# FFN weights as one-byte integers, cast to bf16 by every load, with the zero point taken out by a rank-1 product

## The chip, the cores and the metric

The kernel runs on all 8 NeuronCores of one Trainium2 chip. Each core computes one batch element on its own (2048 tokens of 2048 features), with the same weights. The metric is the device time of the slowest core in microseconds. Cores 0 to 3 are one die, cores 4 to 7 the other. The profile is one execution, read on its slowest core, core 1.

## The reference

One transformer layer with the norm behind each part. B = 8, S = E = 2048, 16 heads, 5632 hidden units. Weights of the FFN are integers 0 to 255 held as int32, with a zero point of 128 and a scale per output row.

```python
# attention (latent kv of 128, 64 plain + 64 rotary dims a head), causal
out  = softmax((q_nope @ k_nope.T + q_rope @ k_rope.T) / sqrt(128)) @ v
x    = layernorm(x + out.reshape(B, S, 2048) @ W_o)
# FFN
def qlinear(x, wq, scale):
    return x @ ((wq.astype(float32) - 128.0) * scale[:, None]).T
h    = silu(qlinear(x, wq_gate, s_gate)) * qlinear(x, wq_up, s_up)
x    = layernorm(x + qlinear(h, wq_down, s_down))
```

## The kernel before

Everything is held transposed: features on the 128 partitions, tokens along the row. The kernel goes through the tokens in four tiles of 512 (`ti` = 0 to 3). A small scheduler, `Sched`, appends each step to a list per engine, with the semaphore counts it waits for; an engine's list is replayed strictly in the order in which the Python code made it. The engines are "t" TensorE (PE), "v" VectorE (DVE), "s" ScalarE (ACT), "g" GpSimd (POOL) and "q" SyncE (SP). DMAs stand in the lists of the engines that issue them: SP and ACT use the hardware queues, POOL the software queue. All matrix products are recorded in one helper (L163), so the profile tells them apart by their tiles.

Preparation (0 to 198 us): small weights are loaded as float32 and cast; `W_o` is cast to bf16 and written to the DRAM scratch `wo_b`.

Each tile then has these stages.

- Start (`emit_astart`, made at the end of the tile before, ahead of its second layer norm). POOL loads x for the tile into `C` as bf16 in two DMAs (L315, from float32), each of 8 x 512 columns; PE makes the latent kv, the latent query and the rotary key from it (`SA<-C,w_dkv` first), then the 16 heads' queries.
- Attention, head by head. For each pair of key blocks, PE puts scores into the PSUM bank pair `SA` or `SB` (on the diagonal with a mask product), ACT takes the exp into `AR` (L545), and PE multiplies it with v into `O` and with ones into `SM` for the row sum. The next head's keys and values are made in between (`KV`, L267, L295). Tile `ti` has 2 (`ti` + 1) pairs a head.
- In tile 0 only, three pieces of `wd` are made ready at the start of every head, 48 in all (`mk_wd_part`). SP loads a piece of up to 2048 columns of int32 into `B` (`B<-wd`, 1024 KB), one buffer for all pieces; DVE (L478, pieces 0 and 2 of a row) or ACT (L481, piece 1) subtracts 128 and writes bf16; ACT issues the store to the scratch `wd_b` (L490). These steps stand in the engines' lists ahead of the head's own exps.
- Output projection from `wo_b`, residual, first layer norm. Its result is in `A` (float32) and in `C` (bf16, cast in four parts by L789).
- Gate/up: 44 chunks `hc` of 128 hidden units, 16 products each for gate and for up, into `SA` and `SB` in turn. L903 is the silu, L912 the product with up, which writes `H[hc]` in `AR`. The weights of a chunk, 128 x 2048 each, have two buffers each in `AR`. In tile 0 POOL loads them from int32 with a cast to bf16 in the DMA (`AR<-wg`, `AR<-wu`, L813 and L819), DVE subtracts 128 in place (L825, L832), and ACT writes them to the scratches `wg_b` and `wu_b`; a buffer is free when both its products and its store are done. In tiles 1 to 3 SP loads bf16 from the scratches.
- Down: 16 groups `ec` of 44 products into `O0` and `O1` in turn. The 5632 columns of a group's weights lie in `AR` in two halves. They are loaded in four pieces: pieces 0 and 1 (2048 and 768 columns) once product 21 of the group before is done, pieces 2 and 3 (1280 and 1536) once that group is. Products 0, 16, 22 and 32 wait for pieces 0 to 3. In all tiles SP loads them from `wd_b` (L938). DVE adds the residual (L966).
- Second layer norm, and the store of y.

`m128b` (one row of -128) and `rowb` (one row of 512, bf16) are there before, and nothing reads them.

Of the kernel before, what the change touches and what calls it, by code (L numbers as in the profile page):

```python
# [9 lines left out]
I32 = mybir.dt.int32  # L10

S = 2048
# [68 lines left out]
def build_program(nc):  # L81
# [11 lines left out]
    wg = nc.dram_tensor("wg", [NHC, 128, NEC * 128], I32, kind="ExternalInput")  # L93
    wu = nc.dram_tensor("wu", [NHC, 128, NEC * 128], I32, kind="ExternalInput")
    wd = nc.dram_tensor("wd", [NEC, 128, NHC * 128], I32, kind="ExternalInput")
# [8 lines left out]
    wg_b = nc.dram_tensor("wg_b", [NHC, 128, NEC * 128], BF16, kind="Internal")  # L104
    wu_b = nc.dram_tensor("wu_b", [NHC, 128, NEC * 128], BF16, kind="Internal")
    wd_b = nc.dram_tensor("wd_b", [NEC, 128, NHC * 128], BF16, kind="Internal")
# [4 lines left out]
    with ExitStack() as ctx:  # L111
# [3 lines left out]
        def ps(name):  # L115
# [32 lines left out]
                     "Dp0", "Dp1", "Dp2", "Dst0", "Dst1", "Dst2", "Dst3",  # L148
                     "Dsg0", "Dsg1", "Dsu0", "Dsu1", "Dsd0", "Dsd1",
                     "Dwo0", "Dwo1", "Dg0", "Dg1", "Du0", "Du1",  # L150
                     "Dd0", "Dd1", "Dy"]
# [4 lines left out]
        pi = [B[:, i * 2048:(i + 1) * 2048].bitcast(I32) for i in range(4)]  # L156
# [65 lines left out]

        piQ = [B[:, i * 2048:(i + 1) * 2048].bitcast(I32) for i in range(4)]
        poQ = B[:, 6144:8192].bitcast(BF16)
        conv_tok = {}
# [17 lines left out]
        tok_expt_rd = [None, None]  # L243
        t_hc_last = None
# [187 lines left out]
        for ti in range(NT):  # L432
# [26 lines left out]
            wd_parts = []  # L459
            if ti == 0:  # L460
                cstate = {"q2": [t for t in half_free if t is not None],
                          "po0": None, "po1": None,
                          "st_wg0": None, "st_wg1": None,
                          "st_wu0": None, "st_wu1": None, "blast": []}

                def mk_wd_part(row, part):
                    def run():
                        w0 = part * 2048
                        n = min(2048, NHC * 128 - w0)
                        t_ld = sc.dma(  # L470
                            "q",
                            lambda q, row=row, w0=w0, n=n: q.dma_start(
                                piQ[2][:, 0:n], wd[row, :, w0:w0 + n]),
                            deps=[cstate["q2"]], inc="Dp0")
                        po = poQ[:, (part % 2) * 2048:(part % 2) * 2048 + n]
                        t_cv = sc.st(
                            "v" if part % 2 == 0 else "s",
                            (lambda v, po=po, n=n: v.tensor_scalar(  # L478
                                po, piQ[2][:, 0:n], -128.0, None, ALU.add))
                            if part % 2 == 0 else  # L480
                            (lambda s, po=po, n=n: s.activation(  # L481
                                po, piQ[2][:, 0:n], AF.Identity,
                                bias=np.float32(-128.0))),
                            deps=[t_ld, cstate["po%d" % (part % 2)]],
                            inc="V" if part % 2 == 0 else "S")
                        cstate["q2"] = t_cv
                        t_st = sc.dma(
                            "s",
                            lambda s, row=row, w0=w0, n=n, po=po:
                            s.dma_start(wd_b[row, :, w0:w0 + n], po),  # L490
                            deps=[t_cv], inc="Dsd%d" % (part % 2))
                        cstate["po%d" % (part % 2)] = t_st
# [631 lines left out]
```

How the kernel before makes its waits and increments, by code:

```python
    def replay(self, eng_name, eng, sems):  # L52
        wm = {}
        for fn, waits, inc, amt in self.steps[eng_name]:
            for (sname, val) in waits:
                if wm.get(sname, 0) < val:
                    eng.wait_ge(sems[sname], val)
                    wm[sname] = val
            inst = fn(eng)
            if inc is not None:
                inst.then_inc(sems[inc], amt)
```

## Time and profile before

| | us |
|---|---|
| median of 2 runs | 4304.75 (4299.38 to 4310.12) |
| the profiled execution, its own time | 4291.6 |
| its span, core 1 | 4290.1 |
| the eight cores' spans | 4260.5 to 4290.1 |
| mean granted clock of the cores | 0.877 to 0.880 of full speed |

The span is the time from the first to the last instruction of the slowest core. In the page and in the answers, a row such as `O<-AR` says what is written and what is read; a releaser behind `<-` is what ended an engine's wait. For a DMA, the row gives the KB written and the time from its issue to its landing. A DMA queue's share is the time that its packets took, as a part of the 16 DMA engines' time.

### The profile page before, as it was taken

To read this page: it belongs to the slowest core of one execution; us is meant where nothing else is said; L and a number is where in the kernel's file an instruction comes from. 1 tells how busy PE (TensorE), PEld (TensorE's weight loads), DVE (VectorE), ACT (ScalarE), POOL (GpSimd) and SP (SyncE) were. 2 spreads that over 40 slices of the span, in tenths; PEclk is the share of its full clock that TensorE was granted. 3 is DMA by queue.
4 is the path that set the end of the run, shared out by engine and by line. 5 is a ranking of instruction groups with operands and counts; after the bars stand their busy time and mean duration, and the time that the engine had idled before them with its cause. 6 is when DMAs were issued, how large, how long until landed. Compare 5 with 4: busy or idle time off the path is not lost.

```text
span 4290.1 us, 35670 instructions; the slowest of 8 cores (4260.5 to 4290.1 us)
## 1 busy us (share of the span) xinstructions
PE 3250.2 (76%) x13312; PEld 1235.0 (29%) x13312; DVE 859.9 (20%) x1275; ACT 846.4 (20%) x985; POOL 56.4 (1%) x100
## 2 busy tenths in 40 slices
PE   0133337677789578799996688799995788889996
PEld 0000002233334122344442122344441222334442
DVE  1031111322211422311004321311004222121102
ACT  1122222100000243210002444210002455211000
POOL 0000000011100000000000000000000000000000
PEclk9955558899999688899997888899996898989998
DMA  6634444699973200344540201344540200234442
GB/s 217 184 119 162 161 162 131 148 216 210 212 185 110 78 2 20 103 152 152 157 150 13 79 1 34 104 152 152 160 144 0 79 1 1 98 118 152 148 150 101
DMA packets 154950, 505.71 MB, mean 118 GB/s; under 512 B 15136, under 2 KB 31648, under 8 KB 147616
## 3 DMA queue, kind: packets, MB, share of 16 engines
q1 hardware_dynamic: 103648, 354.51, 25.2%
q0 software_dynamic: 20992, 54.53, 8.4%
q10 hardware_dynamic: 30144, 94.38, 5.7%
q8 instruction: 112, 1.84, 0.2%
q14 instruction: 54, 0.44, 0.0%
HBM read 463.52 MB, written 94.37 MB: 130 GB/s over the span
## 4 chain that ended last, share of the span: by engine, by line
PE 62%; DMA 19%; DVE 9%; ACT 5%; issue 4%; DVEq 0%; ACTq 0%; SPq 0%; POOL 0%; POOLq 0%
PE O L163 18%; PE SA L163 17%; PE SB L163 16%; PE SM L163 8%; DMA B<-wd 4%; DMA AR<-wu 4%; DMA wu_b<-AR 4%; PE KV L163 3%; DVE A L767 2%; ACT AR L545 2%; DMA B<-wo 1%; DMA wo_b<-C 1%; DVE AR L409 1%; DVE B L775 1%; DMA AR<-wo_b 1%
## 5 line engine op out<-in xcount | busy, mean ns | idle before, releaser
L163 PE MATMUL O<-AR 128*128 128x512 bf16 x3456 | 840.4, 392 | 339.7 <-ACT AR L545 327.2
L163 PE MATMUL SA<-C,AR 128*128 128x512 bf16 x2816 | 647.5, 388 | 135.9 <-DVE AR L825 68.0
L163 PE MATMUL SB<-C,AR 128*128 128x512 bf16 x2816 | 628.7, 381 | 48.2 <-DVE AR L825 45.3
L163 PEld LDWEIGHTS O<-AR 128*128 128x128 bf16 x3456 | 335.8, 100 | 797.3 <-issue 439.2
L163 PEld LDWEIGHTS SA<-C,AR 128*128 128x128 bf16 x2816 | 276.6, 99 | 500.1 <-issue 189.6
L163 PEld LDWEIGHTS SB<-C,AR 128*128 128x128 bf16 x2816 | 274.7, 98 | 391.5 <-issue 70.0
L163 PE MATMUL SA<-AR 128*128 128x512 bf16 x832 | 256.6, 425 | 58.7 <-DVE AR L295 52.9
L163 PE MATMUL SM<-AR,onesb 128*1 128x512 bf16 x640 | 227.6, 443 | 60.9 <-DVE AR L611 60.9
L545 ACT ACTIVATE AR<-SA 128x1024 bf16<-128x1024 f32 x160 | 164.0, 1025 | 415.0 <-PE SA L163 220.5
L163 PE MATMUL SB<-AR 128*128 128x512 bf16 x832 | 234.6, 396 | 9.3 <-DMA AR<-wo_b 5.0
L295 DVE CAST AR<-KV 128x512 bf16<-128x512 f32 x160 | 110.7, 692 | 471.8 <-PE KV L163 471.8
L903 ACT ACTIVATE AR<-SB,sgT 128x512 bf16<-128x512 f32 x88 | 60.7, 689 | 602.8 <-PE SB L163 565.1
L545 ACT ACTIVATE AR<-SB 128x1024 bf16<-128x1024 f32 x160 | 163.0, 1019 | 77.5 <-PE SB L163 74.1
L903 ACT ACTIVATE AR<-SA,sgT 128x512 bf16<-128x512 f32 x88 | 60.7, 689 | 590.5 <-PE SA L163 465.9
L912 DVE SCALAR_TENSOR_TENSOR AR<-SA,suT,AR 128x512 bf16<-128x512 f32 x88 | 66.1, 751 | 515.5 <-PE SA L163 515.5
L912 DVE SCALAR_TENSOR_TENSOR AR<-SB,suT,AR 128x512 bf16<-128x512 f32 x88 | 66.1, 751 | 507.8 <-PE SB L163 507.8
L163 PE MATMUL SA<-C,w_dkv 128*128 128x512 bf16 x64 | 18.0, 441 | 194.6 <-DMA C<-x 194.6
L966 DVE SCALAR_TENSOR_TENSOR B<-O,sdT,A 128x512 f32<-128x512 f32 x64 | 48.1, 751 | 577.8 <-PE O L163 577.8
L163 PEld LDWEIGHTS SA<-AR 128*128 128x128 bf16 x832 | 76.2, 102 | 192.3 <-issue 138.6
L267 ACT CAST AR<-KV 64x512 bf16<-64x512 f32 x160 | 91.6, 573 | 176.6 <-PE KV L163 176.6
L611 DVE COPY AR<-SM 128x512 f32<-128x512 f32 x64 | 44.3, 692 | 361.7 <-PE SM L163 361.7
L163 PE MATMUL SM<-rows,onesf 1*128 1x512 f32 x128 | 85.0, 749 | 36.0 <-ACT rows L596 36.0
(90 smaller groups left out, 1717.1 us busy)
## 6 DMA issues: line engine op xcount, KB each, us to landing
AR<-wg_b SPq DMA_DIRECT2D x132, 512.0 KB, 3.3
AR<-wu_b SPq DMA_DIRECT2D x132, 512.0 KB, 3.3
B<-wd SPq DMA_DIRECT2D x32, 1024.0 KB, 6.3
AR<-wo_b SPq DMA_DIRECT2D x64, 512.0 KB, 3.3
AR<-wd_b SPq DMA_DIRECT2D x64, 512.0 KB, 3.8
AR<-wd_b SPq DMA_DIRECT2D x64, 384.0 KB, 3.7
AR<-wg POOLq DMA_DIRECT2D x44, 512.0 KB, 9.0
AR<-wu POOLq DMA_DIRECT2D x44, 512.0 KB, 9.7
```

The lines of the kernel that those rows point to most:

```text
L163: t.matmul(o, l, r, start=a, stop=b),
L267: lambda s, khs=khs, c5=c5: s.copy(AR[0:64, khs + c5 * 512:khs + (c5 + 1) * 512], KV[0:64, :]),
L295: lambda v, vts=vts, tg=tg: v.tensor_copy(AR[:, vts + tg * 512:vts + (tg + 1) * 512], KV[:, :]),
L409: lambda v, ssl=ssl, b=Pb: v.tensor_tensor(scrB, b[64:128, :], ssl, ALU.mult),
L545: lambda s, SC=SC, etb=etb: s.activation(AR[:, etb:etb + 1024], SC[:, 0:1024], AF.Exp, scale=np.float32(QSCALE)),
L611: "v", lambda v: v.tensor_copy(sbinv, SM[:, :]),
L767: lambda v, ec2=ec2: v.tensor_tensor(dst_f32[:, ec2 * 512:(ec2 + 1) * 512], src_f32[:, ec2 * 512:(ec2 + 1) * 512], O0[:, :], ALU.subtract),
L775: lambda v, ec2=ec2, out_t=out_t: v.tensor_tensor(out_t[:, ec2 * 512:(ec2 + 1) * 512], dst_f32[:, ec2 * 512:(ec2 + 1) * 512], O1[:, :], AL ...
L903: lambda s, hc=hc, pgb=pgb, gsil_o=gsil_o: s.activation(AR[:, gsil_o:gsil_o + 512], pgb, AF.Silu, scale=sgT[:, hc:hc + 1]),
L912: v.scalar_tensor_tensor(AR[:, AR_H + hc * 512:AR_H + (hc + 1) * 512], pub, suT[:, hc:hc + 1], AR[:, gsil_o:gsil_o + 512], ALU.mult, ALU.m ...
L966: lambda v, ec=ec, pbd=pbd: v.scalar_tensor_tensor(B[:, ec * 512:(ec + 1) * 512], pbd[:, :], sdT[:, ec:ec + 1], A[:, ec * 512:(ec + 1) * 512],
```

## The change

The host hands over `wg`, `wu` and `wd` as uint8. The scratches `wg_b`, `wu_b` and `wd_b`, the 48 `wd` steps of tile 0's attention and the DVE subtractions are gone. In all four tiles POOL loads gate, up and down weights with a cast from uint8 to bf16 in the DMA, in one list in the order of use, and the products are made with the raw 0 to 255.

For gate and up nothing takes the place of the subtraction: their input is the output of the layer norm, whose features add up to zero for each token, so a constant of 128 in every weight adds nothing (up to rounding). For down the zero point is taken off with the column sums of `H`: 44 products with a column of ones add them up in `SM[0:1]` (one ahead of each chunk from chunk 2 on, two behind the last), ACT copies them as bf16 to `rowb`, and a rank-1 product of `m128b` and `rowb` closes each of the 16 groups of the down stage.

```diff
-    wg = nc.dram_tensor("wg", [NHC, 128, NEC * 128], I32, kind="ExternalInput")
+    wg = nc.dram_tensor("wg", [NHC, 128, NEC * 128], U8, kind="ExternalInput")
...
-                for _ in range(3):
-                    if wd_parts:
-                        wd_parts.pop(0)()
...
-                if ti == 0:
-                    t_gl = sc.dma(
-                        "g",
...
-                else:
-                    t_gl = sc.dma(
-                        "q",
...
+                t_gl = sc.dma(
+                    "g",
+                    lambda g, hc=hc, gb=gb: g.dma_start(
+                        AR[:, AR_GS[gb]:AR_GS[gb] + 2048],
+                        wg[hc, :, :]),
+                    deps=[t_g_free[gb]], inc="Dg%d" % gb)
...
+                if hc >= 2:
+                    MM(SM[0:1, :], onesb[:, :],
+                       AR[:, AR_H + (hc - 2) * 512:AR_H + (hc - 1) * 512],
+                       hc - 2 == 0, False,
+                       [t_H[hc - 2]] + ([tok_pb["SM"]] if hc == 2 else []))
...
+            t_cs = MM(SM[0:1, :], onesb[:, :],
+                      AR[:, AR_H + 43 * 512:AR_H + 44 * 512], False, True,
+                      [t_H[43]], inc="T")
+            t_rowb = sc.st(
+                "s", lambda s: s.copy(rowb[0:1, :], SM[0:1, :]),
+                deps=[t_cs, tok_rowb_free], inc="S")
...
                     hw[p] = sc.dma(
-                        "q",
-                        lambda q, ec=ec, c0=c0, c1=c1: q.dma_start(
-                            AR[:, c0:c1], wd_b[ec, :, c0:c1]),
-                        deps=pc_dep[p] + [t_d_free[p // 2]]
-                             + (store_tok[("wd_b", ec)] if ti <= 1 else []),
+                        "g",
+                        lambda g, ec=ec, c0=c0, c1=c1: g.dma_start(
+                            AR[:, c0:c1], wd[ec, :, c0:c1]),
+                        deps=pc_dep[p] + [t_d_free[p // 2]],
                         inc=pc_sem[p])
...
+                t_dm = MM(pbd[:, :], m128b[0:1, :], rowb[0:1, :],
+                          False, True, [t_rowb], inc="T")
```

ScalarE, one head of tile 0's attention before (L545 the exps, L591 and L596 the inverse of the row sum, L490 the stores to `wd_b`):

```order
L490 DMA wd_b<-B 128x2048 [waits semV]
L481 ACTIVATE B<-B 128x2048 [waits semDp0,semDsd1]
L490 DMA wd_b<-B 128x2048 [waits semS]
L490 DMA wd_b<-B 128x1536 [waits semV]
L545 ACTIVATE AR<-SA 128x1024 [waits semT]
L591 ACTIVATE rows<-SM 1x512
L596 ACTIVATE rows<-rows 1x512 [waits semS]
L267 CAST AR<-KV 64x512 [waits semT]
L545 ACTIVATE AR<-SB 128x1024 [waits semT]
```

The same head after the change (L494 is now the exp, L540, L545 and L261 the other three):

```order
L494 ACTIVATE AR<-SA 128x1024 [waits semT]
L540 ACTIVATE rows<-SM 1x512
L545 ACTIVATE rows<-rows 1x512 [waits semS]
L261 CAST AR<-KV 64x512 [waits semT]
L494 ACTIVATE AR<-SB 128x1024 [waits semT]
```

The four steps for `wd` ahead of the first exp are gone, the rest stands as it was.

POOL, at the end of tile 0's FFN, before: the last load of `wu`, then x for the tiles 1, 2 and 3 with nothing between.

```order
L819 DMA AR<-wu 128x2048 [waits semT,semDsu1]
L315 DMA C<-x 128x8x512 [waits semV]
L315 DMA C<-x 128x8x512
L315 DMA C<-x 128x8x512 [waits semV]
L315 DMA C<-x 128x8x512
```

After: the last two groups of the down weights of tile 0 (L844), x for tile 1 (L309), and the first weights of tile 1 (L758, L764).

```order
L844 DMA AR<-wd 128x2048 [waits semT]
L844 DMA AR<-wd 128x768
L844 DMA AR<-wd 128x1280 [waits semT]
L844 DMA AR<-wd 128x1536
L309 DMA C<-x 128x8x512 [waits semV]
L309 DMA C<-x 128x8x512
L758 DMA AR<-wg 128x2048 [waits semT]
L764 DMA AR<-wu 128x2048
```

The loads of x now stand behind all 64 pieces of the tile's down weights.

PE, from the last chunk of gate/up into the first down group, after the change (`SM<-AR,onesb` is a column sum of `H`, `O<-rowb,m128b` the rank-1 product):

```order
L159 MATMUL SB<-C,AR 128x512 [waits semDu1]
L159 MATMUL SB<-C,AR 128x512 x15
L159 MATMUL SM<-AR,onesb 1x512 [waits semV] x2
L159 MATMUL O<-AR 128x512 [waits semDd0]
L159 MATMUL O<-AR 128x512 x15
L159 MATMUL O<-AR 128x512 [waits semDd1]
L159 MATMUL O<-AR 128x512 x5
L159 MATMUL O<-AR 128x512 [waits semDd2]
L159 MATMUL O<-AR 128x512 x9
L159 MATMUL O<-AR 128x512 [waits semDd3]
L159 MATMUL O<-AR 128x512 x11
L159 MATMUL O<-rowb,m128b 128x512 [waits semS]
```

Before, the same place has the 32 products of the chunk and then the 44 of the group, without the two column sums and the last row.

## Rows read from the trace of the kernel before

**Rows 1.** The page, part 4: the chain that ended last, shares by line.
```profile
PE O L163 18%; PE SA L163 17%; PE SB L163 16%; PE SM L163 8%; DMA B<-wd 4%; DMA AR<-wu 4%; DMA wu_b<-AR 4%; PE KV L163 3%; DVE A L767 2%; ACT AR L545 2%; DMA B<-wo 1%; DMA wo_b<-C 1%; DVE AR L409 1%; DVE B L775 1%; DMA AR<-wo_b 1%
```

**Rows 2.** Table of stretches: length, busy us (instructions) per engine, granted clock, DMA share, GB/s.
```profile
249.00:678.00 429.00, 158.31 (x362) 35.01 (x362) 70.19 (x91) 85.82 (x94) 0.00 (x0) 0.58 0.48 162
...
777.00:1210.00 433.00, 329.02 (x1409) 136.78 (x1410) 89.52 (x130) 32.87 (x46) 46.89 (x84) 0.96 0.96 210
...
1802.00:2106.00 304.00, 303.66 (x1398) 137.25 (x1399) 32.35 (x44) 31.84 (x46) 0.00 (x0) 0.99 0.44 148
...
4079.00:4231.00 152.00, 152.00 (x706) 68.79 (x704) 12.02 (x16) 0.00 (x0) 0.00 (x0) 1.00 0.43 145
```

**Rows 3.** Waits of PE and ACT in tile 0's attention: us in total, times, longest.
```profile
PE O L163 <- ACT AR L545: 238.1, 16, 16.7
...
ACT B L481 <- DMA B<-wd: 215.4, 16, 14.0
ACT AR L545 <- DVE B L478: 119.3, 16, 7.8
```

**Rows 4.** Timeline of one head in tile 0: start us, us, engine, line.
```profile
576.44 1.91 ACT L481 ACTIVATE B<-B 128x2048 bf16<-128x2048 int32 x1 [13.85 <-DMA B<-wd]
...
584.18 0.96 DVE L478 TENSOR_SCALAR B<-B 128x1536 bf16<-128x1536 int32 x1 [14.47 <-DMA B<-wd]
585.68 1.02 ACT L545 ACTIVATE AR<-SA 128x1024 bf16<-128x1024 f32 x1 [7.33 <-DVE B L478]
...
586.85 1.01 PE L163 MATMUL O<-AR 128*128 128x512 bf16 x2 [15.93 <-ACT AR L545]
```

**Rows 5.** Timeline around the ends of gate/up, tiles 0 and 1.
```profile
776.36 1.91 ACT L789 ACTIVATE C<-A 128x2048 bf16<-128x2048 f32 x1 [3.65 <-DVE A L775]
...
777.12 9.61 PE L163 MATMUL SA<-C,AR 128*128 128x512 bf16 x32 [23.29 <-DVE AR L825]
...
1209.81 9.66 PE L163 MATMUL O<-AR 128*128 128x512 bf16 x44
...
1800.29 1.91 ACT L789 ACTIVATE C<-A 128x2048 bf16<-128x2048 f32 x1 [3.65 <-DVE A L775]
...
2105.59 1.67 PE L163 MATMUL O<-AR 128*128 128x512 bf16 x7
2105.93 0.75 DVE L912 SCALAR_TENSOR_TENSOR AR<-SB,suT,AR 128x512 bf16<-128x512 f32 x1 [6.16 <-PE SB L163]
```

**Rows 6.** POOL's loads: queues from 780 to 1210 us, tile wg, 736.8 to 739.2.
```profile
q0 software_dynamic: 12096, 44.05, 68.2%
q10 hardware_dynamic: 12435, 45.24, 27.7%
...
L813 POOL DMA_DIRECT2D AR<-wg x44: 528/528/853, 736.8 to 1192.4; - x44
...
DMA to landing us min/median/max: 5.2/9.0/13.9
...
DMA packets 0, 0.00 MB, mean 0 GB/s; under 512 B 0, under 2 KB 0, under 8 KB 0
...
AR<-wg POOLq DMA_DIRECT2D x1, 512.0 KB, 6.9
```

**Rows 7.** Waits of PE; down stage of tile 3; SP's issue; packets from 2169 to 2170.6.
```profile
PE O L163 <- DMA AR<-wd_b: 12.5, 6, 5.1
...
AR<-wd_b SPq DMA_DIRECT2D x15, 512.0 KB, 3.9
...
2169.27 0.79 SPq L938 DMA_DIRECT2D AR<-wd_b  x2
...
q1 hardware_dynamic: 3, 0.01, 4.8%
```

**Rows 8.** Timeline, a run of products with one column of weights.
```profile
1768.68 3.62 PE L163 MATMUL KV<-AR,onesb 128*1 128x512 bf16 x16
```

**Rows 9.** DMA queues from 3060 to 3085 us, x for tile 3.
```profile
q0 software_dynamic: 2080, 2.10, 52.7%
```

More of the change, by code:

```diff
@@ L10 @@
 I32 = mybir.dt.int32
+U8 = mybir.dt.uint8
 S = 2048
@@ L457, in build_program @@
                     deps=tok_A_free, inc="Dx%d" % (2 + j)))
-            wd_parts = []
-            if ti == 0:
[L461 to L470, printed above, removed]
-                            "q",
[L472 to L492, printed above, removed]
-                        store_tok.setdefault(("wd_b", row), []).append(t_st)
-                        cstate["blast"] = [t_cv, t_st]
-                    return run
-                for row in range(NEC):
-                    for part in range(3):
-                        wd_parts.append(mk_wd_part(row, part))
             pending_tail = None
@@ L666, in build_program @@
                     deps=[t_mm, t_xr[ec // 8]]
-                         + (tok_B_free if ec == 0 else [])
-                         + (cstate["blast"] + [cstate["q2"], cstate["po0"],
-                                               cstate["po1"]]
-                            if ec == 8 and ti == 0 else []), inc="V")
+                         + (tok_B_free if ec == 0 else []), inc="V")
                 tok_pb[wn] = t_add
@@ new lines, in build_program @@
+                t_gl = sc.dma(
[4 more added lines that the diff above has]
+                    deps=[t_g_free[gb]], inc="Dg%d" % gb)
+                t_ul = sc.dma(
+                    "g",
+                    lambda g, hc=hc, gb=gb: g.dma_start(
+                        AR[:, AR_US[gb]:AR_US[gb] + 2048],
+                        wu[hc, :, :]),
+                    deps=[t_u_free[gb]], inc="Du%d" % gb)
@@ L894, in build_program @@
                 ums.append(t_um)
-                if ti == 0:
-                    t_g_free[gb] = [t_gm, st_g]
-                    t_u_free[gb] = [t_um, st_u]
-                else:
-                    t_g_free[gb] = t_gm
-                    t_u_free[gb] = t_um
+                t_g_free[gb] = t_gm
+                t_u_free[gb] = t_um
                 t_sil = sc.st(
@@ L957, in build_program @@
                               AR[:, AR_H + hc * 512:AR_H + (hc + 1) * 512],
-                              hc == 0, hc == NHC - 1, d,
-                              inc="T" if hc in (21, NHC - 1) else None)
+                              hc == 0, False, d,
+                              inc="T" if hc == 21 else None)
                     if hc == 21:
                         t_d_free[0] = t_dm
+                t_dm = MM(pbd[:, :], m128b[0:1, :], rowb[0:1, :],
+                          False, True, [t_rowb], inc="T")
+                tok_rowb_free = t_dm
                 t_d_free[1] = t_dm
@@ L1063, in _host_layouts @@
         wo.reshape(16, 128, 16, 128).transpose(2, 1, 0, 3).reshape(16, 128, 2048))
-    wgq = np.asarray(inputs["L0_ffn_wq_gate"], np.int32).T
+    wgq = np.asarray(inputs["L0_ffn_wq_gate"], np.int32).astype(np.uint8).T
     d["wg"] = np.ascontiguousarray(
         wgq.reshape(16, 128, 44, 128).transpose(2, 1, 0, 3).reshape(44, 128, 2048))
-    wuq = np.asarray(inputs["L0_ffn_wq_up"], np.int32).T
+    wuq = np.asarray(inputs["L0_ffn_wq_up"], np.int32).astype(np.uint8).T
     d["wu"] = np.ascontiguousarray(
         wuq.reshape(16, 128, 44, 128).transpose(2, 1, 0, 3).reshape(44, 128, 2048))
-    wdn = np.asarray(inputs["L0_ffn_wq_down"], np.int32).T
+    wdn = np.asarray(inputs["L0_ffn_wq_down"], np.int32).astype(np.uint8).T
     d["wd"] = np.ascontiguousarray(
```

97 lines of the change are left out of this document (14 added, 83 removed).

## The prediction

> **What bounds the kernel now.** I read the page first, its chain that ended last. The products of TensorE (PE, line L163) lead it, but `B<-wd`, `AR<-wu` and `wu_b<-AR` stand in it with 4% of the span each, 12% together [rows 1]. All three belong to the dequantisation, so the next view is the table of stretches, to see where PE has holes [rows 2]. Gate/up of tile 0 takes 433 us with the 16 DMA engines at 0.96, where the same matmuls take about 304 us with DMA at 0.44 in tile 1. Attention of tile 0 takes 429 us with PE busy for 158. The down products are packed (152 of 152 us in tile 3).
>
> The waits of PE in tile 0's attention name one thing: 238.1 us, 16 times, once a head, until the exp of L545 [rows 3]. ScalarE itself is late because it stands at L481 for the `wd` load (215.4 us) and then, in the first exp, for L478 (119.3 us) [rows 3]. The timeline of one head shows it: L481 begins at 576.44 when its load has landed, the second store sits on ScalarE's queue until L478 has run at 584.18, and the exp starts at 585.68 [rows 4]. So attention of tile 0 is bounded by three serial load-convert rounds a head.
>
> **What goes.** (a) The 48 `wd` rounds. The 16 waits of 238.1 us go. What is late next is the exp itself, which lets PE go 1.17 us after its own start (585.68 to 586.85), most of it under the other bank's score products; I leave 0.4 us of wait a head, 6.4 us. A head is 429 / 16 = 26.8 us now, so 26.8 - 15.9 = 10.9 us without the wait of the row, at a granted clock of 0.58 of full speed on average [rows 2, 4]. With fewer holes the clock should be higher, so a little comes on top: 238 - 6 + 6 = **238 us**, between 225 and 256.
>
> (b) Gate/up of tile 0. I measure from one anchor, the last cast of the normalised tile (L789), to the first down product: 776.36 to 1209.81 is 433.5 us in tile 0, 1800.29 to 2105.59 is 305.3 us in tile 1 [rows 5]. The int32 load plus the bf16 write-back fill the engines: 68.2% + 27.7% of 430 us [rows 6]. That is 430 x 0.682 / 84 = 3.49 us of all 16 engines a load and 430 x 0.277 / 86 = 1.39 a store; two of each make 9.76 us a chunk, where PE needs 6.91 (32 products at 0.216). With the stores, the L825/L832 steps and three quarters of the source bytes gone, tile 0 runs as tile 1: **-128 us**.
>
> (c) PE waits 12.5 us in all for `wd_b` pieces at the start of the down stage [rows 7], while in tiles 0 to 2 x for the next tile is loaded beside them (in tile 3, without it, PE is busy throughout [rows 2]). The x load moves away: **-12.5 us**, at worst 0.
>
> **What comes.** (d) 44 column-sum products and 16 rank-1 products a tile, 240 in all. One-column products of this width stand 3.62 us for 16, less the tail of the last [rows 8]: 0.216 us each, the same as a full one (44 in 9.66 with the last one's tail, [rows 5]). Nothing hides them, since PE is packed here: 240 x 0.216 = **+52 us**.
>
> (e) The last column sum needs `H[43]`. L912 begins 0.34 us after the last up product is over and takes 0.75 [rows 5]; before, 43 down products lay over this. About 1 us, 4 times: **+4 us**. The row copy on ScalarE has the whole first down group as cover (9.5 us).
>
> (f) Loads of the gate/up stage leave SP's hardware queue for POOL's software queue, with the cast in the DMA. POOL issues one in 0.53 us [rows 6]. Each buffer is free for three half chunks, 10.4 us, before it is needed. A landing of 6.9 us (software, first pair, [rows 6]) is hidden. Even if the cast still cost 3.49 us a load, two would take 6.98 us of a chunk's 6.91 + 0.22 = 7.13. **0 us**, at most some 20.
>
> (g) The down stage has much less cover. Pieces 0 and 1 of the next group can be issued when product 21 is done, and piece 0 is needed after 22 more products and the rank-1 one: 23 x 0.216 = 4.97 us. The time from one group to the next is thus at least 4.75 us plus the landing. The hardware queue lands piece 0 in 3.9 us in tile 3 [rows 7], where PE is busy throughout [rows 2]. The software queue starts later: its first load was issued at 736.8, no packet moved until 739.2 (2.4 us) and it landed after 6.9 [rows 6]; on SP, issued at 2169.27, the first packets are there before 2170.6 (under 1.3 us) [rows 7]. That is 1.1 us or a little more between the two, 1.2. So 3.9 + 1.2 + 0.1 for the semaphores = 5.2 us, if uint8 to bf16 costs what a bf16 load of as many written bytes costs. Bounds: 3.9 (nothing lost) to 6.9 us (the int32 load of 1 MB in the first pair). I take 5.2, since the bytes written are those of the rows of the down stage. Lost: 4.75 + 5.25 - 9.72 = 0.3 us a group, 63 groups: **+19 us**; with the bounds 0 and 123 us.
>
> The Trainium skill, DMA: Bandwidth & Descriptors, section "Anatomy of one DMA", gives about 2.0 us plus bytes / 436e3 for a software-queue DMA, 3.2 us for piece 0. By that, (g) would be 0 and the sum 19 us lower. The trace does not agree: 2.4 us passed before the first packet. The same page (section "Latency and other measured facts") puts the software queue's first byte only 0.4 us behind the hardware one; the rows have 1.2 us between them.
>
> (h) `C<-x` of the next tile was issued as soon as `H[43]` was there, and lay under the whole down stage. Now its two DMAs stand on POOL behind 64 `wd` pieces, and the last two of these wait for the end of group 14. They go out two issues of 0.53 us, 1.1 us, into group 15. PE's next work (L163 `SA<-C,w_dkv`) is behind group 15 and needs the first half of x, then the second. With nothing else moving, the pair for tile 3 took 52.7% of 16 engines over 25 us, 13.2 us of transfer [rows 9]. Counted from the start of group 15: 1.1 + 2.4, one more for pieces 2 and 3 in front, then 13.2 to 15: the second half is there at 18 to 20 us, and PE would have needed it at 9.7 + 1.7 = 11.4. Three times about 8 us, 24. After such a hole the clock is at its lower level for a while: after the 23 us hole at 777.12 a run of 32 products took 9.61 us where 32 x 0.216 + 0.15 is 7.06 [rows 5], 2.6 us more. **+32 us**, between 15 and 45.
>
> **The sum** against the profiled execution (span 4290.1, its own time 4291.6): -238 - 128 - 12.5 + 52 + 4 + 0 + 19 + 32 = -271.5, so 4020 us. The two runs shown have a median 13 us above the profiled one; with part of that I say **4030 us**. HBM traffic falls (each weight is read as one byte, never written), but no row shows HBM as a limit outside tile 0, so I book nothing for it.
>
> **Rivals.** *The cast costs by element.* If the DMA engines spend the same time on 262,144 elements whether these are int32 or uint8, a load stays at 3.49 us, where the bf16 loads of tile 1 take 0.44 x 304 / 88 = 1.52 [rows 2]. For: only 4-byte sources are cast in this trace, and nothing shows one with a 1-byte source. Against: bytes read explain 3.49 as well (1 MB). Then (f) holds at its edge and piece 0 lands at about 6.3 us: 4.75 + 6.35 - 9.72 = 1.4 us a group, 87 in place of 19: **4098 us**.
>
> *The software queue keeps its slow landing* (median 9.0 us [rows 6]) in the down stage. Then a group takes 4.75 + 9.0 = 13.8 us, 4 more than now, 255 us in all: **4266 us**, within 2%. This is also the way to a slower kernel: place, the down stage; price, 63 us for each us of landing over 4.97; from a landing of about 9.6 us nothing is left of the gain, and the 13.9 us that is the row's maximum would end at **4577 us**. For: same queue, same engine. Against: these 9 us were taken with DMA at 0.96, with stores and int32 sources that are gone; in the down stage the share is about 0.43.
>
> *Attention of tile 0 does not shrink*, because the wait only changes hands. For: ScalarE carries the exps, and the waits of one engine are rarely due to one other alone. If only half of the 238 us came back: **4150 us**. Against: all three parties of the wait are removed instructions.
>
> **How the numbers follow.** Forecast 0.72, cast by element 0.15, half of attention's gain 0.05, slow landing at 9 us 0.04, slower still 0.02, something better (no late x, no late piece, near 3980) 0.02. A change of about 2% is what can be told from none here. Faster by over 2% (below 4219): 0.72 + 0.15 + 0.05 + 0.02 + a little = 0.95; within 2%: 0.03; slower: 0.02. The range of 3975 to 4125 takes in the element rival and the bounds of (g) and (h).
>
> **What would show it.** In the profile after: tile 0's attention at some 11 us a head with no `B<-wd`; gate/up of every tile 6.91 + 0.22 us a chunk; PE waits for `AR<-wd` small and many (0.3 us x 60) or, for the element rival, 1.4 us each; PE waits for `C<-x` three times 6 to 10 us before `SA<-C,w_dkv`. If DMA's share in gate/up of tile 1 is near 0.45 the cast goes by bytes, near 0.98 by elements. I am wrong if the software queue lands pieces later than 6.9 us, or if tile 0's heads stay above 15 us.

## The result, and the profile after

The changed kernel takes 3995.66 us (median of 11 executions) against 4305.76 us (10 executions) for the kernel before. The ratio is 0.9285, 95% interval 0.9264 to 0.9306: 7% faster. The forecast was 4030 us, with a range of 3975 to 4125 us; the median lies in it. Ratios are taken from executions in which no die ran at a lower granted clock than the other; where the chip showed that in most executions of a kernel (e7), single undisturbed ones are named instead.

The page's first line and its chain that ended last, by line (changed kernel):
```profile
span 3991.4 us, 35128 instructions; the slowest of 8 cores (3964.9 to 3991.4 us)
...
PE SA L159 22%; PE SB L159 20%; PE O L159 19%; PE SM L159 10%; PE KV L159 4%; DVE A L713 2%; DMA C<-x 2%; ACT AR L494 2%; DVE AR L289 1%; DMA B<-wo 1%; DMA wo_b<-C 1%; DVE AR L403 1%; DVE A L721 1%; DVE B L721 1%; DVE AR L560 1%
```

The three transfers that held 12% of the chain [rows 1] are gone from it. Of the DMA that is left there, `wo` and 27 us of `C<-x` belong to the start of the kernel, which the change does not touch. The rest of `C<-x` is new: the chain runs through a load of x at the start of each of the tiles 1, 2 and 3 (14.8, 14.7 and 14.0 us), which is term (h).

The table of stretches, changed kernel (columns as in [rows 2]): attention of tile 0, gate/up of tile 0, gate/up of tile 1, down of tile 3:
```profile
246.00:405.80 159.80, 124.30 (x353) 32.30 (x357) 35.19 (x59) 55.30 (x78) 0.00 (x0) 0.72 0.02 7
501.50:826.80 325.30, 320.74 (x1413) 137.42 (x1443) 33.03 (x44) 33.51 (x47) 46.51 (x88) 0.99 0.41 141
1423.00:1748.40 325.40, 320.78 (x1413) 137.45 (x1443) 33.02 (x44) 33.53 (x47) 46.53 (x88) 0.99 0.41 140
3773.30:3931.90 158.60, 157.74 (x706) 68.94 (x720) 11.26 (x15) 0.53 (x1) 31.79 (x60) 1.00 0.42 137
```

Tile 0's attention, up to the first product of the output projection (405.82 us), is down from 429 to 160 us, 10.0 us a head, and its gate/up from 433 to 325 [rows 2]. But gate/up of tile 1 went up from 304 to 325, with PE busy for 320.8 of it, and down of tile 3 from 152 to 158.6, with PE busy for 157.7. These two rows say that the added products cost more than their number times 0.216 us. The timeline of PE shows how:

Timeline of PE, changed kernel, two chunks in tile 0, the end of gate/up, and two down groups of tile 3 (start us, us, engine, line):
```profile
788.50 0.38 PE L159 MATMUL SM<-AR,onesb 128*1 128x512 bf16 x1
788.81 7.08 PE L159 MATMUL SB<-C,AR 128*128 128x512 bf16 x31
...
795.82 0.38 PE L159 MATMUL SM<-AR,onesb 128*1 128x512 bf16 x1
...
826.25 0.38 PE L159 MATMUL SM<-AR,onesb 128*1 128x512 bf16 x1 [0.77 <-DVE AR L811]
826.78 8.58 PE L159 MATMUL O<-AR 128*128 128x512 bf16 x39 [0.16 <-issue]
...
3911.65 0.39 PE L159 MATMUL O<-rowb,m128b 1*128 1x512 bf16 x1
3911.97 9.67 PE L159 MATMUL O<-AR 128*128 128x512 bf16 x43
3921.57 0.39 PE L159 MATMUL O<-rowb,m128b 1*128 1x512 bf16 x1
```

From one column sum to the next are 795.82 - 788.50 = 7.32 us, where 32 products take 6.91 us: 0.41 us for the one that was added. (The records hold 31 of the 32 here, so the period is the thing to read, not the count.) From one rank-1 product to the next are 3921.57 - 3911.65 = 9.92 us where 44 products take 9.50: 0.42 us. The wait of 0.77 us at 826.25 is term (e).

The waits of PE in two stretches (us in total, times, longest), and the tiles `wd` and `wg`, changed kernel; first the largest of PE in tile 0's attention, then the whole from 200 us on:
```profile
PE SM L159 <- DVE AR L560: 15.1, 15, 1.0
...
PE SA L159 <- DMA C<-x: 15.5, 6, 3.2
...
PE SM L159 <- DVE AR L811: 3.1, 4, 0.8
...
DMA to landing us min/median/max: 2.3/3.3/4.7
...
DMA to landing us min/median/max: 3.1/3.4/3.8
```

The 238.1 us until the exp [rows 3] are gone altogether: no row of PE in tile 0's attention names the exp. No row of PE names `AR<-wd` either: the four pieces of the down weights together land in 3.3 us (median, at most 4.7) and are never waited for. `C<-x` is waited for twice at each of the three tile starts.

Where the time went, stage by stage, in the two profiled executions (anchors as in the prediction, [rows 5]):

| stretch | before | after | difference | forecast |
|---|---|---|---|---|
| up to the use of the second half of x in tile 0 | 198.2 | 194.5 | -3.6 | 0 |
| tile 0: start, attention, projection, norm | 578.2 | 307.0 | -271.2 | -238 |
| tile 0: gate/up | 433.5 | 325.3 | -108.2 | -128 + 9.5 + 1 |
| tiles 1 to 3: gate/up | 915.2 | 973.9 | +58.7 | 28.5 + 3 |
| four down stages | 626.1 | 634.6 | +8.5 | -12.5 + 13.8 + 19 |
| tiles 1 to 3: attention, with the wait for x; tail | | | +17 | +32 |

(28.5 is 3 x 44 x 0.216, 13.8 is 64 x 0.216.) The differences add up to -299, as the spans do: 4290.1 - 3991.4 = 298.7. The first row is work that the change leaves alone. Of the second row, 269 us lie ahead of the output projection; from the first product of the projection to the end of the norm it is 98.0 us before and 95.7 after.

### The profile page after: what moved, and what is told of

Read it like the earlier page. It is cut to its first block, busy times and chain, and to the rows that moved or that the text cites. A ratio compares the mean times of both kernels' runs of the same rounds, so it can differ in the third digit from the quotient of the medians.

```text
span 3991.4 us, 35128 instructions; the slowest of 8 cores (3964.9 to 3991.4 us)
## 1 busy us (share of the span) xinstructions
PE 3274.0 (82%) x13289; PEld 1236.0 (31%) x13552; DVE 766.8 (19%) x1155; ACT 817.2 (20%) x973; POOL 329.2 (8%) x620
## 4 chain that ended last, share of the span: by engine, by line
PE 75%; DVE 9%; DMA 6%; ACT 5%; issue 4%; DVEq 0%; POOL 0%; ACTq 0%; another core or an unknown queue 0%; SPq 0%; POOLq 0%
PE SA L159 22%; PE SB L159 20%; PE O L159 19%; PE SM L159 10%; PE KV L159 4%; DVE A L713 2%; DMA C<-x 2%; ACT AR L494 2%; DVE AR L289 1%; DMA B<-wo 1%; DMA wo_b<-C 1%; DVE AR L403 1%; DVE A L721 1%; DVE B L721 1%; DVE AR L560 1%
## 5 line engine op out<-in xcount | busy, mean ns | idle before, releaser
L159 PE MATMUL O<-AR 128*128 128x512 bf16 x3376 | 828.3, 388 | 95.4 <-ACT AR L494 89.0
L159 PE MATMUL SA<-C,AR 128*128 128x512 bf16 x2756 | 639.3, 387 | 80.5 <-ACT C L735 77.8
L159 PE MATMUL SB<-C,AR 128*128 128x512 bf16 x2760 | 620.1, 379 | 2.9
L159 PEld LDWEIGHTS SA<-C,AR 128*128 128x128 bf16 x2816 | 271.2, 99 | 430.5 <-issue 130.0
L159 PE MATMUL SM<-AR,onesb 128*1 128x512 bf16 x816 | 289.3, 422 | 65.3 <-DVE AR L560 60.5
L159 PE MATMUL SA<-AR 128*128 128x512 bf16 x803 | 246.0, 420 | 64.0 <-DVE AR L289 52.2
L758 POOL DMA_DIRECT2D AR<-wg x176 | 93.1, 529 | 2409.6 <-PE SA L159 2106.4
L494 ACT ACTIVATE AR<-SA 128x1024 bf16<-128x1024 f32 x160 | 163.9, 1024 | 393.8 <-PE SA L159 318.1
L844 POOL DMA_DIRECT2D AR<-wd x256 | 135.5, 534 | 526.3 <-PE O L159 477.6
L494 ACT ACTIVATE AR<-SB 128x1024 bf16<-128x1024 f32 x160 | 162.8, 1018 | 76.8 <-PE SB L159 76.5
L159 PEld LDWEIGHTS SM<-AR,onesb 128*1 128x1 bf16 x816 | 42.9, 80 | 320.8 <-issue 320.8
```

Of the source, the lines that this page charges most:

```text
L159: t.matmul(o, l, r, start=a, stop=b),
L494: lambda s, SC=SC, etb=etb: s.activation(AR[:, etb:etb + 1024], SC[:, 0:1024], AF.Exp, scale=np.float32(QSCALE)),
L758: lambda g, hc=hc, gb=gb: g.dma_start(AR[:, AR_GS[gb]:AR_GS[gb] + 2048], wg[hc, :, :]),
L844: lambda g, ec=ec, c0=c0, c1=c1: g.dma_start(AR[:, c0:c1], wd[ec, :, c0:c1]),
```

## The experiments

Two theories stood against each other at first. Mine: the gain is two separate things, the `wd` rounds and the engines' load in gate/up, and the price is what the added products cost on a packed PE. The rivals: the gains hang together (one saves nothing without the other), or the price lies in the software queue or in late x.

Where a run is so many us below the changed kernel, its median is taken from 3995.66 us. The two were not always timed side by side, so the difference of their ratios to the kernel before, in us and with its interval, stands beside it where it matters.

**e1: the down weights alone.** They come as uint8 through POOL, the `wd` rounds are gone; gate and up are converted as before.

```
-    wg = nc.dram_tensor("wg", [...], U8, ...)
+    wg = nc.dram_tensor("wg", [...], I32, ...)
...
+    wg_b = nc.dram_tensor("wg_b", [NHC, 128, NEC * 128], BF16, kind="Internal")
...
+                if ti == 0:
+                    t_g_free[gb] = [t_gm, st_g]
```

> The kernel before with the down weights alone changed: uint8 cast on load by POOL, no wd rounds in tile 0's attention; gate/up as before (int32, -128 on DVE, scratches), no column sums and no rank-1 products, so the zero point of the down weights is left out. Theory (terms read from the profile after): attention of tile 0 -260 us, output projection and norm of tile 0 -11 us, the waits for wd_b pieces -12, late x +20: about 4305 - 263 = 4042 us, ratio 0.939. Rival, the sizes of the prediction: -238 - 12.5 + 19 + 32 = -200, 4105 us, ratio 0.953.

Measured: 4032.23 us, ratio 0.9396 (0.9362 to 0.943). Table of stretches of e1, attention and gate/up of tile 0:
```profile
246.00:408.00 162.00, 129.59 (x360) 33.08 (x357) 35.20 (x59) 55.26 (x78) 0.00 (x0) 0.69 0.02 7
524.00:948.00 424.00, 320.73 (x1356) 133.08 (x1355) 87.85 (x126) 28.97 (x43) 47.55 (x86) 0.95 0.97 210
```
Attention of tile 0 shrinks as far as in the changed kernel (the stretch of 162 us against 429) while gate/up stays at 424 us with the engines at 0.97. So the `wd` rounds are a gain by themselves. The ratio meets the expectation (0.939); its rival, the sizes of the prediction (0.953), lies outside the interval.

**e2: gate and up alone.** They come as uint8 through POOL in all tiles; the `wd` rounds and the bf16 copy of `wd` stay.

```
-    wd = nc.dram_tensor("wd", [NEC, 128, NHC * 128], U8, kind="ExternalInput")
+    wd = nc.dram_tensor("wd", [NEC, 128, NHC * 128], I32, kind="ExternalInput")
...
+                for _ in range(3):
+                    if wd_parts:
+                        wd_parts.pop(0)()
```

> The kernel before with the gate/up weights alone changed: uint8 cast on load by POOL in all tiles, no subtraction on DVE, no scratches for them; the wd rounds in tile 0's attention and the down stage as before. Theory: gate/up of tile 0 falls to the 305 us of tile 1, -128 us, all else stays: 4177 us, ratio 0.970. Rival: the software queue costs something in tiles 1 to 3 (cast by element, landing over 10.4 us), then gate/up there is longer than 305 us and the ratio is above 0.98.

Measured: ratio 0.9707 (0.9616 to 0.9798); the profiled execution has 4146.6 us. Table of stretches of e2, gate/up of tile 0 and tile 1:
```profile
775.00:1080.60 305.60, 302.62 (x1368) 137.29 (x1397) 32.28 (x43) 32.88 (x46) 44.38 (x84) 0.99 0.44 147
1668.00:1972.00 304.00, 301.74 (x1367) 137.04 (x1396) 32.27 (x43) 32.16 (x46) 44.38 (x84) 0.99 0.44 148
```
Its waits of PE still hold the exps, 310.5 us in 69 waits where the kernel before has 327.2 in 72. Tile 0's gate/up, from the last cast to the first down product, needs 306.2 us (774.46 to 1080.64) in place of 433.5: -127 us, term (b) as forecast. Tile 1, where only the queue changed (POOL with a cast in place of SP), stays at 304: term (f), nothing, is right too. The two halves are independent, and the spans of the profiled executions say so once more: e1 is 4290.1 - 4036.8 = 253 us shorter than the kernel before and e2 143.5 us, 397 together, and the whole change without its added products (e3, below) is 396 us shorter.

**e3: without the added products.** Column sums and rank-1 products are left out, and with them the zero point of the down weights.

```
-                    MM(SM[0:1, :], onesb[:, :],
-                       AR[:, AR_H + (hc - 2) * 512:AR_H + (hc - 1) * 512],
...
-                t_dm = MM(pbd[:, :], m128b[0:1, :], rowb[0:1, :],
-                          False, True, [t_rowb], inc="T")
```

> The changed kernel without its 44 column sums and 16 rank-1 products a tile; the zero point of the down weights is left out. Theory: each inserted product costs 0.41 us with the switch to another shape and back, so 240 of them 98 us, and the wait for H[43] 4: about 3894 us, ratio to before 0.905. Rival (the prediction's price, 0.216 us each): 52 + 4 = 56 us, about 3940 us, ratio 0.915.

Measured: 3894.53 us, ratio 0.9076 (0.9046 to 0.9107), 101 us below the changed kernel; by the ratios 90 us, 16 either way, by the two profiled spans 97. The rival's 56 us is out. The wait for `H[43]` went with the products, so of the 101 us some 94 are theirs, about 0.4 us each and not 0.216. Gate/up of tile 0 in e3:
```profile
507.00:812.00 305.00, 302.89 (x1395) 136.93 (x1396) 32.26 (x43) 33.48 (x46) 46.52 (x88) 0.99 0.44 148
```

**e4: the column sums in one run.** The same 44 products, all behind the last up product and not one in each chunk.

```
-            MM(SM[0:1, :], onesb[:, :],
-               AR[:, AR_H + 42 * 512:AR_H + 43 * 512], False, False,
...
+            for hc in range(NHC):
+                t_cs = MM(SM[0:1, :], onesb[:, :],
+                          AR[:, AR_H + hc * 512:AR_H + (hc + 1) * 512],
```

> The changed kernel with all 44 column sums of a tile in one run behind the last chunk, in place of one ahead of each chunk; same products, same result. Switch theory (the extra 0.2 us is paid where the shape or the bank changes, about 0.1 at each end): 44 in a run stand at 0.216, so 42 x 0.2 x 4 = 33 us less than the changed kernel, about 3963 us, chunk period 6.91. Rival, shape theory (a one-column product itself costs 0.41 in this stage): nothing changes, 3996 us. What the wait for H[43] was stays.

Measured: 3954.16 us, ratio 0.9218 (0.9197 to 0.9239), 41 us below the changed kernel with the same number of products (by the ratios 29 us, 13 either way, so clear of the rival's nothing). Timeline of PE in e4:
```profile
799.75 7.07 PE L159 MATMUL SB<-C,AR 128*128 128x512 bf16 x32
806.75 9.66 PE L159 MATMUL SM<-AR,onesb 128*1 128x512 bf16 x44
816.34 9.67 PE L159 MATMUL O<-AR 128*128 128x512 bf16 x44
825.94 0.39 PE L159 MATMUL O<-rowb,m128b 1*128 1x512 bf16 x1
```
The 44 take 9.6 us, 0.22 each. Back to back with their like they cost what I had charged; it is the single one among others that costs 0.41. From 7.07 us for 32 to the next start are 7.00, not 6.91, and 9.59 for 44 in place of 9.50: each change of shape costs some 0.1 us. One part of the expectation missed: the wait for `H[43]` did not stay. No idle time stands in the run of 44, whose first 43 need only earlier chunks. Gate/up of the four tiles is 39 us shorter in all, 33 from the changes of shape and 6 from this.

**e5: the rank-1 product at full height.** `rowb` and `m128b` get 128 rows (127 of `rowb` zero), so that the closing product has the shape of the others.

```
-        m128b = sb("m128b", [1, 128], BF16)
-        rowb = sb("rowb", [1, 512], BF16)
+        m128b = sb("m128b", [128, 128], BF16)
+        rowb = sb("rowb", [128, 512], BF16)
...
-                t_dm = MM(pbd[:, :], m128b[0:1, :], rowb[0:1, :],
+                t_dm = MM(pbd[:, :], m128b[:, :], rowb[:, :],
```

> The changed kernel with the product that closes a down group in full shape: 128 rows of -128 as weights and a 128-row operand that is zero but for its first row, so the same result. Shape theory for the closing product: a product on one row costs 0.42 us in a run of full ones, a full one 0.216, so a group falls from 9.92 to 9.72 us and the kernel by 64 x 0.2 = 13 us, about 3983 us. Rival: the cost lies in what follows it (the wait for rowb, the change of bank between groups, which groups had before too), then a group stays at 9.92 us.

Measured: 3986.52 us, ratio 0.9252 (0.921 to 0.9294), 9 us below the changed kernel. Timeline of PE in e5:
```profile
3906.20 0.38 PE L159 MATMUL O<-rowb,m128b 128*128 128x512 bf16 x1
3906.42 9.66 PE L159 MATMUL O<-AR 128*128 128x512 bf16 x44
3915.91 0.38 PE L159 MATMUL O<-rowb,m128b 128*128 128x512 bf16 x1
```
A group is 9.71 us, not 9.92: the closing product is 0.2 us cheaper with 128 rows than with one. 64 x 0.2 is 13 us. The total alone could not show it: the medians are 9 us apart, the ratios 14 us with 20 either way. The groups also change between the PSUM banks `O0` and `O1`, and 9.71 us is 45 x 0.216, so the change of bank adds nothing here. So of the 0.42 us half is the product and half the change of shape.

**e6: the down weights as int32.** Same program, only the source type differs: every `wd` piece reads four times the bytes.

```
-    wd = nc.dram_tensor("wd", [NEC, 128, NHC * 128], U8, kind="ExternalInput")
+    wd = nc.dram_tensor("wd", [NEC, 128, NHC * 128], I32, kind="ExternalInput")
```

> The changed kernel with the down weights as int32 again, cast by the load: same bytes written, four times the bytes read, so that the landing of piece 0 gets longer in the quiet down stage. Packets of such a cast took 324 ns in the gate/up stage before, against 175 ns now from uint8. By the prediction's relation for a group (4.75 us + landing + a little): with a landing of 3.5 + 1.375 x 8 x 0.15 = 5.2 us, a group takes 10.0 to 10.2 us in place of 9.92, PE waits 0.1 to 0.3 us a group, 6 to 18 us in all, about 4005 us. Rival 1: software queue slow whenever the source is int32 (2.4 us to the first packet, landing 6.9 as in the first pair before): group 11.7 us, 1.8 x 63 = +112, about 4108 us. Rival 2: the source's width costs nothing: 3996 us.

Measured: ratio 0.9546 (0.9461 to 0.9631), the profiled execution 4115.7 us. Down stage of tile 3 in e6, its landings, its waits, and a piece of its timeline:
```profile
3872.00:4056.00 184.00, 162.03 (x721) 68.95 (x720) 11.26 (x15) 0.58 (x1) 31.70 (x60) 0.99 0.72 120
...
AR<-wd POOLq DMA_DIRECT2D x15, 512.0 KB, 5.6
...
PE O L159 <- DMA AR<-wd: 88.6, 68, 2.9
...
4011.95 9.66 PE L159 MATMUL O<-AR 128*128 128x512 bf16 x44 [1.23 <-DMA AR<-wd]
4023.07 4.91 PE L159 MATMUL O<-AR 128*128 128x512 bf16 x22 [1.14 <-DMA AR<-wd]
4029.35 1.02 PE L159 MATMUL O<-AR 128*128 128x512 bf16 x4 [1.37 <-DMA AR<-wd]
```
A group takes 184 / 16 = 11.5 us, and the price against the changed kernel is 4115.7 - 3991.4 = 124 us. By my relation (4.75 us plus the landing of piece 0) a landing of 5.6 us gives 10.4 us a group, and the expectation worked out on it was missed. The relation counts only the first pair of pieces; the timeline shows PE waiting in the second half of a group too, since the pair behind lands late as well. So the relation is a lower bound. The waits for pieces name 88.6 us of the 119 by which the four down stages grew; for the rest nothing is named. The rival's total comes near the measured one, but by another route: piece 0 lands after 5.6 us, and the second pair adds waits of its own. The experiment shows two things: the landing is the term that decides in the down stage, as the slow rivals had it, and the small source is what kept the changed kernel away from it.

**e7: x in pieces between the down groups.** One sixteenth of x behind each group's four `wd` pieces, and not two large DMAs behind all of them.

```
+                if ti + 1 < NT:
+                    t_x1 = sc.dma(
+                        "g",
+                        lambda g, ec=ec, q1=(ti + 1) * TT: g.dma_start(
+                            C[:, ec * 512:(ec + 1) * 512], ...
```

> The changed kernel with x for the next tile loaded in 16 blocks, one behind the four pieces of each down group, in place of two DMAs behind all 64 pieces. Theory: PE's two waits for C<-x at the start of tiles 1 to 3 (15.5 us in all) and the run at the lower clock behind them go, 20 us together, while a block of 0.5 us of transfer a group is hidden under the pieces: about 3976 us. Rival: each block delays the pieces behind it and PE waits for AR<-wd again, by up to 0.5 us a group, 24 us over three tiles: 3996 us or above.

Measured: 3981.7 and 3982.2 us in its two undisturbed executions, 14 us below the changed kernel; the spans of the profiled executions, 3980.6 and 3991.4, are 11 us apart. Timeline of PE at the start of tile 1, and waits of PE, in e7:
```profile
989.73 0.39 PE L159 MATMUL O<-rowb,m128b 1*128 1x512 bf16 x1
990.05 3.63 PE L159 MATMUL SA<-C,w_dkv 128*128 128x512 bf16 x16
...
PE SA L159 <- DMA C<-x: 192.1, 2, 187.5
PE O L159 <- DMA AR<-wd: 4.0, 3, 1.3
```
In the changed kernel the same place reads:
```profile
985.27 0.38 PE L159 MATMUL O<-rowb,m128b 1*128 1x512 bf16 x1
987.92 1.89 PE L159 MATMUL SA<-C,w_dkv 128*128 128x512 bf16 x8 [2.27 <-DMA C<-x]
...
992.98 2.69 PE L159 MATMUL SA<-C,w_dkv 128*128 128x512 bf16 x8 [3.17 <-DMA C<-x]
995.46 4.55 PE L159 MATMUL SA<-C,w_dq 128*128 128x512 bf16 x15
999.84 2.32 PE L159 MATMUL SB<-C,w_krp 128*128 128x512 bf16 x10
```
The wait for x is gone at the tile starts (the two left are the kernel's own start), 4.0 us of waiting for pieces came for it. So a small part of the rival came true as well: the down stages of tiles 0 to 2 take 159.8 us in place of 158.4, and the gain is 11 to 14 us, not the 20 that were expected.

**e8: the sum on VectorE.** VectorE adds each `H` chunk to `hsum` in f32, the last addition writes `rowb`, and the full-height rank-1 product sums over the partitions. No column sum on PE.

```
+                    t_hs = sc.st(
+                        "v",
+                        lambda v, hsl=hsl, o=(hsum if hc < NHC - 1 else rowb):
+                        v.tensor_tensor(o[:, :], hsum[:, :], hsl, ALU.add),
...
-                t_dm = MM(pbd[:, :], m128b[0:1, :], rowb[0:1, :],
+                t_dm = MM(pbd[:, :], m128b[:, :], rowb[:, :],
```

> The changed kernel with H summed over the 44 chunks on DVE in float32 (an add of 128 x 512 a chunk, last one into bf16), and one full product of 128 rows of -128 with that sum as the close of each down group; no column sums on PE. Theory: chunk period back to 6.91 us (44 x 4 x 0.41 = 72 us), group 9.72 in place of 9.92 (13 us), wait for H[43] gone (4 us): about 3907 us, ratio 0.908. DVE is busy for 0.75 us of a chunk of 6.9, so the add is hidden. Rival: DVE's adds between SBUF operands hold up POOL's software queue or the silu/up chain, loads land late and PE waits for AR<-wg: gain under 40 us.

Measured: 3908.56 us, ratio 0.9066 (0.901 to 0.9121), and timed a second time ratio 0.9073 (0.9041 to 0.9104): 87 us below the changed kernel (by the ratios 94, 25 either way; expected 89). Table of stretches (gate/up of tile 0) and timeline of e8:
```profile
504.00:808.50 304.50, 301.16 (x1368) 136.98 (x1397) 61.79 (x86) 33.25 (x46) 46.50 (x88) 0.99 0.44 149
...
642.78 7.07 PE L160 MATMUL SA<-C,AR 128*128 128x512 bf16 x31
...
643.98 0.69 DVE L824 TENSOR_TENSOR hsum<-hsum,AR 128x512 f32<-128x512 f32 x1
...
649.69 7.07 PE L160 MATMUL SB<-C,AR 128*128 128x512 bf16 x31
```
The chunk is back at 6.91 us. VectorE pays 0.69 us a chunk and stays at 62 us of 304.5.

**e9: e7 and e8 together.** Both edits as above.

> The changed kernel with both edits: H summed on DVE and closed by a full product, and x loaded in 16 blocks among the down pieces. Theory: the gains add, since one is in the gate/up and down groups and the other at the start of tiles 1 to 3: 87 us (run e8_sum_on_dve) and 12 to 14 us (run e7_x_split), about 3895 us, ratio 0.905. Rival: with the shorter groups (9.72 us) the blocks of x and the pieces come late, PE waits for AR<-wd, and the sum is no better than e8_sum_on_dve alone, 3908 us.

> The kernel of run e8_sum_on_dve once more, beside e9_both on the same chip: 3905 us, and the difference to e9_both is the worth of the split load of x, 12 us by theory, 0 by the rival.

Measured: e9 3889.75 us, ratio 0.9029 (0.8999 to 0.906), the fastest of all and 106 us below the changed kernel; e8 beside it on the same chip at ratio 0.9073 (0.9041 to 0.9104). Side by side, the split load of x is worth 17 to 19 us by medians and ratios, a little over the 12 to 14 of the expectation; the profiled spans are 3909.0 and 3888.3 us, and e9 has no wait for x at the tile starts. The rival's nothing is out. The two edits add up: 87 and some 18 us.

## Why the prediction was right, and where its terms were off

The direction and the size were right for the reasons given: e1 and e2 take the two halves of the change apart, each gives its share, and both rows that the prediction read as the bound moved as it said. That the total is only some 30 us off is in part luck: (a), (c), (g) and (h) came out 33, 6, 19 and 16 us better than booked, and (d) and (e) 47 and 3 us worse.

**(a), 238 us, measured 271.** The mechanism held: no wait for the exp is left, not even the 6.4 us that I had kept. The rest is the clock, for which I booked 6 us. Over tile 0's attention PE's busy time was 158.3 us at a mean granted clock of 0.58 [rows 2] and is 124.3 us at 0.72, 34 us less for the same products (a few of their records are missing). 238 + 34 = 272, of which 269 were measured in attention and 2 behind it. That the clock is what made the products shorter is read from the two traces; no run held it apart from the holes.

**(b), 128 us, right** (e2). The 108 us in the table are 128 less tile 0's own column sums.

**(c), 12.5 us, measured 18.** PE waits for no `wd` piece. Before, the down stages took 159.5, 158.9, 154.9 and 151.7 us, so the first three together were 18 us longer than three times the last; 12.5 us of it were named as waits. Now all four take 158.2 to 158.5 us, which is 151.7 and 16 rank-1 products at 0.42. For the other 5.6 us no cause is shown.

**(f), right.** The gate/up loads land in 3.4 us with 10.4 us of cover. The rival that the cast costs by element is out: it wanted DMA near 0.98 in gate/up of tile 1, and the row shows 0.41. That is below the 0.44 of before [rows 2] only because the stage is longer: 0.41 x 325.4 / 88 and 0.44 x 304 / 88 are both 1.52 us of all 16 engines a load.

**(d), 52 us, measured about 99: the step that failed.** "One-column products of this width stand 3.62 us for 16 ... 0.216 us each" was read from a run of 16 of one shape and charged to single products among others. For the rank-1 product no row was read at all. Measured: 176 x 0.41 + 64 x 0.42 = 99 us; with (e) that makes 106, and e3, which leaves both out, gives 101. e4 and e5 show that half of it is the change of shape: the column sum costs 0.22 us among its like (e4), and the closing product 0.21 us when it has the full shape (e5).

The trace of the kernel before held the price already, in the attention of tile 3, where pairs of one-column products stand among full ones at full clock. Its timeline of PE:
```profile
3407.42 0.59 PE L163 MATMUL SM<-AR,onesb 128*1 128x512 bf16 x2
3407.94 0.61 PE L163 MATMUL SB<-AR 128*128 128x512 bf16 x2
3408.39 0.59 PE L163 MATMUL O<-AR 128*128 128x512 bf16 x2
3408.91 0.59 PE L163 MATMUL SM<-AR,onesb 128*1 128x512 bf16 x2
```
Two products take 0.43 us. From full ones to full ones (3407.94 to 3408.39) the step is 0.45 us; from one-column ones to full ones (3407.42 to 3407.94) and the other way (3408.39 to 3408.91) it is 0.52.

**(e), 4 us, measured about 7.** Gate/up grew by (20.0 + 58.7) / 4 = 19.7 us a tile, 20.0 being 128.2 - 108.2; less 44 x 0.41 = 18.0 leaves 1.7. The row names 3.1 us of it as waits.

**(g), 19 us, measured 0.** I took 5.2 us for the landing, from 3.9 on the hardware queue and 1.2 for the software queue's later start. Piece 0 lands in 3.5 us in the down stage of tile 3:
```profile
AR<-wd POOLq DMA_DIRECT2D x15, 512.0 KB, 3.5
```
Why it takes 0.4 us less than the same bytes written did from bf16 on the hardware queue stays open. The 1.2 us were wrong for this source; they had been read from one load of int32. The first packets:

DMA in the changed kernel, two short stretches behind POOL's issue at 463.98 us of a uint8 load:
```profile
DMA packets 0, 0.00 MB, mean 0 GB/s; under 512 B 0, under 2 KB 0, under 8 KB 0
...
q0 software_dynamic: 23, 0.09, 16.5%
...
AR<-wg POOLq DMA_DIRECT2D x1, 512.0 KB, 3.2
```
The first row ends at 465.2 us, the second at 465.5: the first packet comes 1.2 to 1.5 us behind the issue, not 2.4. In e1, which loads the same tile at the same place from an int32 source, it comes 2.6 to 2.9 us behind (issue at 467.49, nothing of this queue before 470.1, packets before 470.4), and the load lands after 6.7 us:
```profile
q0 software_dynamic: 10, 0.04, 12.0%
...
AR<-wg POOLq DMA_DIRECT2D x1, 512.0 KB, 6.7
```
So the delay that I had put down to the queue is not the queue's. It is not simply the source's either. On core 1 of e1 the first load is issued at 463.34 us and has packets before 464.7, 1.4 us behind or less, from the same int32 source. Over the eight cores, the first packet of the first `wg` load comes 1.2 to 1.7 us behind its issue on five cores of e1 and 2.6 to 2.8 us on three; in the kernel before it is four cores (1.2 to 1.4) and four (2.5 to 2.6). From uint8 it is 1.25 us on all eight. The 2.4 us that the prediction read on core 1 was thus one of two values that stood in the same trace; what decides between them is open. What goes with the source is the landing: 4.9 to 7.2 us from int32 on the sixteen cores, 4.9 to 5.9 where the first packet is early, against 3.2 to 3.5 from uint8.

The Trainium skill, DMA: Bandwidth & Descriptors, section "Anatomy of one DMA", gives an estimate of 3.2 us for the 512 KB of piece 0; the pieces here have 3.5. For a one-byte source the page is the better guide than my term was; for the int32 source of e6, with the same bytes written, the rows have 5.6, and the page's figure does not hold.

**(h), 32 us, measured 16.** The two waits stand where the prediction put them, `C<-x` before `SA<-C,w_dkv`, 15.5 us in six waits; the tiles' starts are 6.7, 6.1 and 3.5 us longer. I had x land in 18 to 20 us from the start of group 15; the second half was used at 992.98, 17.5 us after group 15 began (975.51). The wait was not one hole: the first half of x was used at 987.92, so PE waited 2.3 us for it and 3.2 us for the second. Behind them the granted clock is 0.69 and then 0.79: 8 products take 995.46 - 992.98 = 2.5 us where 1.7 is the full rate, the 16 behind them 999.84 - 995.46 = 4.4 where it is 3.5, 1.7 us in all in place of the 2.6 that I had taken from one hole of 23 us. e7 takes this cost away and gains 11 to 14 us.

**Rivals.** Half of attention's gain: out, the wait did not change hands. Slow landing: out, the maximum is 4.7 us. e6 shows, though, that its mechanism is real: 5.6 us of landing already cost 124 us, more than the prediction's relation says.

Against 4020 us, the sum's own result, the profiled execution is 27 us shorter (own time 3993): (a) -33, (c) -6, (d) +47, (e) +3, (g) -19, (h) -16 make -24. The start of the kernel, which the change leaves alone, was 3.6 us shorter. That leaves nothing over.

## What to carry to other kernels

Where TensorE is packed, count the changes of shape and not only the products: a single odd product among full ones costs about twice its slot, so collect them in a run (e4: 41 us), give them the full shape (e5), or hand the sum to an engine with holes (e8: 87 us). Weights kept as one byte and cast by the DMA are cheap in time as well as in traffic, but read the landing from a load with the same source type. And when a queue gets more work, look at what stood behind that work: two large DMAs in the last place cost 15.5 us of waits, sixteen small ones in between 4 us.

## What the runs showed of the hardware

- A one-column product (128*1 weights) between full ones adds 0.41 us, in a run of 44 of its like 0.22 (e4). A one-row product (1*128) between full ones adds 0.42 us, the same sum at full shape 0.21 (e5). A run of one-row products and other shapes were not tried. Why the change costs some 0.1 us at either end stays open.
- On POOL's queue, the first packet of the first `wg` load came 1.25 us after the issue from a uint8 source, on all eight cores. From an int32 source it came after 1.2 to 1.7 us on nine cores and after 2.5 to 2.8 on seven (the kernel before and e1, eight cores each). The cause is open.
- With the same bytes written, a `wd` piece landed in 3.5 us from uint8 and 5.6 us from int32. The 60 loads of tile 3's down stage took 0.42 x 158.6 = 67 us of all 16 engines from uint8 and 0.72 x 184 = 132 us from int32. A gate/up load took 1.52 us of them from uint8 with the cast and 1.52 from bf16 without it. So for sources of 1, 2 and 4 bytes an element and 2 written the time goes as 1, 1 and 2. That fits a price by the larger of the bytes read and written, and not one by the elements; no run tells it from other rules.
